# Folding a random-feature map into its projection weights on one core: head by head in the two halves of the array

## What is computed

```python
q = (x @ Wq.T + bq).reshape(Bx, Sx, H, D)
k = (x @ Wk.T + bk).reshape(Bx, Sx, H, D)
v = (x @ Wv.T + bv).reshape(Bx, Sx, H, D)
q = q / jnp.linalg.norm(q)
k = k / jnp.linalg.norm(k)

def phi(t):
    sq_norm = jnp.sum(t * t)
    scale = jnp.exp(-sq_norm / 2) / jnp.sqrt(jnp.float32(M))
    return jnp.exp(jnp.einsum('hmd,bshd->bshm', weights, t)) * scale
phi_q = phi(q)
phi_k = phi(k)
s = jnp.einsum('bshm,bshm->bsh', phi_q, phi_k)[..., None]
out = s * v / s
```

## Time and profile before

| | us |
|---|---|
| median of 3 runs | 1732.07 (1731.98 to 1737.02) |
| the profiled execution, its own time | 1732.95 |
| its span in the trace | 1730.1 |
| PE busy (share of the span) | 1671.7 (97%) |
| PEld busy | 1350.5 (78%) |
| DVE busy | 1096.4 (63%) |
| ACT busy | 521.7 (30%) |
| POOL busy | 585.3 (34%) |

### The profile page before, as it was taken

The page is one execution under the profiler, slowest core; times in us unless marked ns, Lnnn a source line. Parts: engine busy times, 40 slices in busy tenths (PEclk is TensorE's granted clock), DMA queues, the critical chain, the costliest instruction groups (busy, mean ns, idle before and its releaser), DMA issues.

```text
span 1730.1 us, 23534 instructions
## 1 busy us (share of the span) xinstructions
PE 1671.7 (97%) x8070; PEld 1350.5 (78%) x8070; DVE 1096.4 (63%) x2542; ACT 521.7 (30%) x619; POOL 585.3 (34%) x392
## 2 busy tenths in 40 slices
PE   5899999999999999999999999999999999998897
PEld 5799988877888888888877777787877878875565
DVE  6776554466667866656666664485674865846764
ACT  4442310322222111114222222233332333333443
POOL 2011566787776777777667100000000000000000
PEclk9999999999999999999999999999999999999999
DMA  9998988445686765557877646245345453453455
GB/s 298 355 401 324 315 243 254 119 99 112 161 199 164 201 141 136 137 155 182 239 206 205 182 151 198 91 136 141 95 137 137 141 140 92 143 134 94 138 160 165
DMA packets 159268, 307.99 MB, mean 178 GB/s; under 512 B 60386, under 2 KB 95250, under 8 KB 159208
## 3 DMA queue, kind: packets, MB, share of 16 engines
q1 hardware_dynamic: 89572, 227.66, 41.8%
q0 software_dynamic: 61824, 52.62, 14.8%
q10 hardware_dynamic: 7812, 26.97, 5.1%
HBM read 205.95 MB, written 101.24 MB: 178 GB/s over the span
## 4 chain that ended last, share of the span: by engine, by line
PE 91%; DVE 4%; DMA 2%; ACT 1%; issue 1%; ACTq 0%; SPq 0%; DVEq 0%
PE PS L363 23%; PE PS L364 23%; PE PS L362 23%; PE PS L1347 4%; PE PS L1348 4%; PE PS L1349 4%; PE PS L1557 4%; PE PS L1582 2%; PE PS L1407 2%; DMA xnT<-XT 1%; DMA Aside<-A_dense 1%; DVE stats L976 1%; ACT hqT L942 1%; PE PS L1364 0%; PE PS L1327 0%
## 5 line engine op out<-in xcount | busy, mean ns | idle before, releaser
L695 POOL DMA_INDIRECT A_dense<-wtot,cell x336 | 542.2, 1614 | 225.1 <-DMA A_dense<-wtot,cell 133.5
L363 PE MATMUL PS<-SH,AL 125*125 125x512 f32 x784 | 309.6, 395 | 0.0
L364 PE MATMUL PS<-SH,AH 125*125 125x512 f32 x784 | 309.4, 395 | 0.0
L362 PE MATMUL PS<-SL,AH 125*125 125x512 f32 x784 | 307.9, 393 | 0.2 <-DVE AL L1183 0.2
L362 PE MATMUL PS<-WL,xtH 128*125 128x512 f32 x640 | 252.6, 395 | 0.0
L363 PE MATMUL PS<-WH,xtL 128*125 128x512 f32 x640 | 251.7, 393 | 0.0
L364 PE MATMUL PS<-WH,xtH 128*125 128x512 f32 x640 | 251.3, 393 | 0.0
L1181 DVE TENSOR_TENSOR SL<-S,SH 125x1024 fp32r<-125x1024 f32 x98 | 119.9, 1223 | 167.3 <-ACT SH L879 167.3
L879 ACT ACTIVATE SH<-S 125x1024 fp32r (+1 forms) x98 | 103.9, 1061 | 317.1 <-PE PS L364 317.1
L362 PEld LDWEIGHTS PS<-SL,AH 125*125 125x125 f32 x784 | 145.4, 185 | 38.8 <-DVE AL L1183 1.6
L363 PEld LDWEIGHTS PS<-SH,AL 125*125 125x125 f32 x784 | 145.7, 186 | 36.4
(11 more groups left out here) (182 smaller groups left out, 2560.0 us busy)
## 6 DMA issues: line engine op xcount, KB each, us to landing
A_dense<-zeros POOLq DMA_DIRECT2D x40, 1280.0 KB, 8.5
xt<-xnT SPq DMA_DIRECT2D x60, 500.0 KB, 5.9
Araw<-A_dense SPq DMA_DIRECT2D x100, 250.0 KB, 2.7
Aside<-A_dense SPq DMA_DIRECT2D x100, 250.0 KB, 2.9
keyrow<-key_rows SPq DMA_DIRECT2D x42, 512.0 KB, 4.0
ewrow<-weight_rows SPq DMA_DIRECT2D x42, 512.0 KB, 5.6
xnT<-XT ACTq DMA_DIRECT2D x20, 500.0 KB, 9.0
rt<-r SPq DMA_DIRECT2D x22, 448.0 KB
```

What stands on the lines that cost most here:

```text
L362: nc.tensor.matmul(o, lh, rl, start=start, stop=False)
L363: nc.tensor.matmul(o, ll, rh, start=False, stop=False)
L364: return nc.tensor.matmul(o, lh, rh, start=False, stop=stop)
L695: pool.indirect_dma_start(cells[m], bass.IndirectOffsetOnAxis(cell[:, col:col + 1], 0), wtot[:, col:col + 1], None, compute_op=ALU.add).th ...
```

## The change

The fold of the 1024 columns is made head by head. Each product over 128 rows and 128 moving columns becomes two products of 64 rows and 64 moving columns: one for the upper head of the pair, on partitions 0 to 63 of `raw` and `bdqk`, and one for the lower head, on partitions 64 to 127. Both have 128 stationary columns. The first goes to the slot's first bank, the second to its second bank, and there head pair j has columns 64 j to 64 j + 63. So the columns of a slot stand in another order in PSUM, and ACT's and DVE's reads (`folded`) and their views of `TH` and `TL` (`by_head`) put them back: what lies in `TH` and `TL` is as before. The products that were left out are those with the zero blocks. The bias keeps its form (`fold_bias`), and so do all waits and semaphores.

```diff
+    def by_head(ap):
+        return ap.rearrange("p (j b n) -> p j b n", b=2, n=HD)
+
+    def folded(slot):
+        return PS[:, 4 + 2 * slot:6 + 2 * slot, :].rearrange("p b (j n) -> p j b n", n=HD)
...
-            nc.scalar.activation(TH[:, k, :], two_banks(2 + k % 2), ACT.Copy).then_inc(s_fh, 1)
+            nc.scalar.activation(by_head(TH[:, k, :]), folded(k % 2), ACT.Copy).then_inc(s_fh, 1)
...
-            nc.vector.tensor_tensor(TL[:, k, :], two_banks(2 + k % 2), TH[:, k, :].bitcast(F32), ALU.subtract).then_inc(s_fl, 1)
+            nc.vector.tensor_tensor(by_head(TL[:, k, :]), folded(k % 2), by_head(TH[:, k, :].bitcast(F32)), ALU.subtract).then_inc(s_fl, 1)
...
-        def fold(lhs_of, rows, slot):
+        def fold(k, slot):
             for j in range(KT):
-                if rows == P and slot == 0:
+                if slot == 0:
                     pe.wait_ge(s_bdq, 4 if j >= KT // 2 else 2)
                 for m in range(2):
-                    last = nc.tensor.matmul(by_block(two_banks(2 + slot))[0:rows, j, :], lhs_of(m * KT + j), bdqk[:, m, j, :],
+                    for h in range(2):
+                        half = slice(h * HD, (h + 1) * HD)
+                        last = nc.tensor.matmul(PS[:, 4 + 2 * slot + h, j * HD:(j + 1) * HD],
+                                                raw[half, m * KT + j, k * P:(k + 1) * P], bdqk[half, m, j, half],
+                                                start=m == 0, stop=m == 1)
+            last.then_inc(s_fold, 1)
+
+        def fold_bias():
+            for j in range(KT):
+                for m in range(2):
+                    last = nc.tensor.matmul(by_block(two_banks(2))[0:2, j, :], raw[:, m * KT + j, D:EXT], bdqk[:, m, j, :],
                                             start=m == 0, stop=m == 1)
             last.then_inc(s_fold, 1)
...
-            fold(lambda n: raw[:, n, k * P:(k + 1) * P], P, k % 2)
+            fold(k, k % 2)
         pe.wait_ge(s_fl, KT - 1)
-        fold(lambda n: raw[:, n, D:EXT], 2, 0)
+        fold_bias()
```

## The result

The changed kernel takes 1757.91 us (median of 4 runs, 1756.76 to 1759.32) against 1733.52 for the kernel before on the same chip (4 runs, 1731.98 to 1737.02): 1.0138 times as long, 95% interval 1.0119 to 1.0157. It is slower by some 24 us.

A forecast was written before the change was run, and what follows sets the result against it. PE was taken to bound the kernel, with fold loads and products at 0.112 us each; -0.2 us (fold) and +0.2 us (tiling change) left the profiled 1732.95 us unchanged, carried to the median as 1732.0 us, range 1729.0 to 1762.0.

The forecast's parts named there:

- What bounds the kernel, and both load and product at 0.112 us: Fold on PE: loads and products each take 0.112 us, and the fold's length goes into the time one for one.
- Which I take, the halves side by side: Fold: both halves load and multiply in parallel, loads as the bound, 28.4 us against 28.64, a change of -0.2 us.
- Rival A: Fold: weights load one half after the other, 512 x 0.109 us, +27.4 us, 1759.5 us; chance 0.31.
- The clock at the map stage, taken at 0: Start of the map stage: a stretch at 1.2 GHz costing 1.5 us may shift, -1.5 to +1.5 us, taken at 0.
- rival D: Fold: granted clock of 0.50 between 300 and 330 us, blamed on half rows, 1760 us at least; chance 0.03.
- Rival B: Fold: a half does not load while it multiplies, 0.165 us per load and product, 42.2 us, 1745.9 us; chance 0.11.
- Rival C: Fold: loads don't bind, ACT and DVE set 2.1 us per block, -11.8 us, 1720.3 us; chance 0.06.
- ACT and DVE read in runs of 64 at no cost: ACT's copies and DVE's subtractions in the fold: same element counts in runs of 64 across two banks, costed at nothing.
- Tiling change, +0.2 us: Fold on PE: one more change of the array between halves and the bias's form, some 0.2 us (0.1 to 0.3).
- the forecast of no change: Whole kernel: 1732.0 us, anything within 0.3% (5.2 us) counted as no change; chance 0.49.

The follow-up runs named there:

- the warmed version: The changed kernel with 6 unused products of 512 columns in PE's idle time ahead of the fold: 1731.66 us, then 1733.04 us over 12 runs.
- with the wait: The kernel before, with PE starting column block 4 of the fold only when `TL` of block 3 is there: 1738.50 us.
- with the bias first: The kernel before with bias products ahead of the last column block and the first map tile waiting for each `TL` block by itself: 1730.91 us.

## Why the prediction was wrong, point by point

- *What bounds the kernel, and both load and product at 0.112 us:* right. Whole rows with 64 moving columns need twice the loads and cost 0.11 us a load at the full clock, as much as with 128 moving columns; halving the loads' columns as well moved the bound to ACT and DVE. One reading beside it is wrong: PEld does hold more than one load per 0.108 us elsewhere in the trace, where the operands are bf16 (L1543: loads of 128 columns 0.055 us apart from 1575.8 us on). For the F32 loads of the fold and of the Gram stage, which the sums use, it holds.
- *Which I take, the halves side by side:* right. 0.112 us a pair at the fold's start, and 28.73 and 28.80 us for the fold in the two profiles of the warmed version, where the prediction said 28.4 at the full clock. The Trainium skill's statement in "TensorEngine Tiling (Array Packing)", Key Properties, that different tiles can load and multiply in parallel, agrees with the pairs. Rival A gave 1759.5, nearly the time that was measured, by a mechanism that did not occur: the average of 0.105 us a load is 0.213 us a pair at 1.2 GHz. Its sign, copies 7 us apart, came nearly true (6.83) for the same reason.
- *The clock at the map stage, taken at 0, and rival D, chance 0.03:* this is the step that failed. The prediction looked at one fall of the clock, priced it at 1.5 us, and let it move by 1.5 either way; that fall stayed what it was. The idle 1.6 us ahead of the fold stood in the rows it used, and nothing was asked about what a fall there would cost a fold with short products. Rival D named the low clock and priced it nearly rightly (+28 us and more, 1760 at least; the range left most of it out), but gave it the wrong cause, half rows, and argued against it with a stretch from 24 to 56 us. That stretch shows that PE with waits can *keep* the full clock; it says nothing of whether short products can win it back. The clock's term, set to 0, measured +26.0 us: 25.0 in the 512 products (53.82 against 32.45 less the bias fold's 3.60), 1.0 in the bias fold. With the clock held up by the extra products it measured nothing (1733.04 against 1733.53 us).
- *Rival B:* refuted. It wanted 0.165 us from one load of a half to the next, and they are 0.112 us apart at the full clock. The Trainium skill's rule in "TensorE: Matmul & The Clock Gate", section The mechanism, that a load overlaps running products only where its row group differs, therefore holds for neither form of the array here. The same section also names a background weight buffer as a case in which a load is pulled ahead, which rival B left out; what refutes the rival does not tell which of the two happens.
- *Rival C:* its condition (loads below 0.09 us) was not met by the change. It was also set too high: for ACT and DVE to make the pace at 2.1 us per block of 32 pairs, a pair has to take less than 0.066 us. Made true by shorter loads (0.059 us a pair), it gave 1724.4 where 1720.3 was reckoned.
- *ACT and DVE read in runs of 64 at no cost:* right, 1.02 and 1.23 us as before.
- *Tiling change, +0.2 us:* not told apart; the warmed fold of 28.73 us bounds it.
- *Range and chances:* 1757.9 lies inside 1729 to 1762, because A was given 0.31; the forecast of no change, 0.49, did not come true. D, the case that happened in kind, had 0.03.

What stays open: the fall itself. All five profiles of the change and its variants without the extra products ahead show it, between 0.5 us before the fold's start and 2.4 us after; of the three profiles of the fold before without them (as it was, with the wait, with the bias first) two do; of the six profiles of any version with them none does, so without an idle time there the fall was never seen, and with one not always. Whether short products make it likelier was not separated from where the idle time happens to lie.

## What to carry to other kernels

A clock that is down is not a fixed cost. Behind an idle time, look at what the work there does with a low clock: here products of 128 columns beside loads of 128 had it back after 3.4 us, a loss of 1.7 to 1.8 us of time, and products of 64 columns beside the same loads had it for their whole length and took nearly twice as long (6.8 us a block against 3.6). Six products from operands at hand in the idle time mended that, at no cost that 12 runs show (1733.04 against 1733.53 us). And cutting these products' moving columns below their loads' columns gained nothing, in halves or not: count the loads' columns first.

## What was not expected of the hardware

- The clock's state lasted with the short products, in either direction: 1.00 for 28.6 us (warmed), 0.50 for 52.6 us of them and 2.0 us of the bias fold (the change, 302.4 to 357.0) and 0.50 for more than 100 us (whole rows), with PE busy 100% by the profile in each.
- Loads and products of the two halves start together and cost one: 0.112 us a pair at 2.4 GHz, 0.213 at 1.2, for loads of 64 rows and 128 columns; with 64 columns in load and product a pair takes 0.059 us at 2.4 GHz.
- An average rate can hide the clock: 512 loads in 53.6 us are 0.105 us each, close to the full clock's 0.109 for loads in turn. Only the granted clock beside it tells the two apart.
